# A perceiver stack on one core: the last stage's routing, gather and expert loop written anew

## What is computed

```python
logits = x_flat @ router_w
probs = jax.nn.softmax(logits, axis=-1)
expert_idx = jnp.argmax(probs, axis=-1)
gate = jnp.take_along_axis(probs, expert_idx[:, None], axis=1)[:, 0]
onehot = jax.nn.one_hot(expert_idx, E, dtype=jnp.float32)
pos_all = jnp.cumsum(onehot, axis=0) - 1.0
...
keep = (pos < C).astype(x_flat.dtype)
expert_in = expert_in.at[expert_idx, pos_c].add(x_flat * keep[:, None])
hidden = jax.nn.gelu(jnp.einsum('ecd,edf->ecf', expert_in, w1))
expert_out = jnp.einsum('ecf,efd->ecd', hidden, w2)
y = expert_out[expert_idx, pos_c] * (gate * keep)[:, None]
```

## Time and profile before

| | us |
|---|---|
| median of three runs | 3121.58 |
| the three runs | 3120.87, 3121.58, 3126.13 |
| the profiled execution's own time | 3123.37 |
| its span, first to last instruction | 3121.6 |
| PE busy | 2864.2 (92%) |
| DVE busy | 1296.2 (42%) |
| ACT busy | 973.7 (31%) |
| POOL busy | 258.0 (8%) |
| mean granted TensorE clock | 0.958 of full |

### The profile page before, as it was taken

One profiled execution on the slowest core, in us unless ns is written; L12 is line 12 of the kernel. 1 busy time (PEld: TensorE's weight loads), 2 busy tenths in 40 slices (PEclk: granted clock), 3 DMA queues, 4 the chain that ended last, 5 costly groups with the idle time before them and its releaser, 6 DMA issues.

```text
span 3121.6 us, 36422 instructions
## 1 busy us (share of the span) xinstructions
PE 2864.2 (92%) x15622; PEld 1990.0 (64%) x15622; DVE 1296.2 (42%) x1968; ACT 973.7 (31%) x1468; POOL 258.0 (8%) x267
## 2 busy tenths in 40 slices
PE   7977899898898799999999969999999999987887
PEld 3335446356583488888888847877877877844422
DVE  4355463557630633333333334254244244346211
ACT  3233223125331343343433323243233233232110
POOL 1110110221000000000000011101101101000000
PEclk9988999998899899999999979999999999988899
DMA  8872894951021122222222210100100110021197
GB/s 358 305 278 96 327 378 181 362 194 49 14 98 51 55 108 95 95 98 104 95 95 95 94 45 21 45 24 21 44 25 21 44 40 13 17 115 49 70 421 295
DMA packets 63051, 385.16 MB, mean 123 GB/s; under 512 B 6144, under 2 KB 12544, under 8 KB 33328
## 3 DMA queue, kind: packets, MB, share of 16 engines
q1 hardware_dynamic: 26640, 190.57, 16.2%
q0 software_dynamic: 29776, 188.15, 15.6%
q10 hardware_dynamic: 6480, 4.20, 0.4%
HBM read 377.63 MB, written 5.26 MB: 123 GB/s over the span
## 4 chain that ended last, share of the span: by engine, by line
PE 78%; DVE 9%; DMA 6%; ACT 5%; issue 2%; POOL 1%; SPq 0%; DVEq 0%; ACTq 0%; POOLq 0%
PE PS L420 10%; PE PS L422 10%; PE PS L421 10%; PE PS L299 4%; PE PS L607 4%; PE PS L1692 4%; PE PS L1673 3%; PE PS L580 3%; PE PS L1656 3%; PE PS L1675 3%; PE PS L1674 3%; PE PS L1658 3%; PE PS L1657 3%; DMA ring<-in_experts 2%; PE PS L1709 2%; DMA PR<-in_ctxN 2%
## 5 line engine op out<-in xcount | busy, mean ns | idle before, releaser
L420 PE MATMUL PS<-X_high,W_high 128*128 128x512 f32 x576 | 226.6, 393 | 11.0 <-DVE X_low L1151 11.0
L421 PE MATMUL PS<-X_low,W_high 128*128 128x512 f32 x576 | 225.8, 392 | 0.0
L422 PE MATMUL PS<-X_high,W_part 128*128 128x512 f32 x576 | 225.8, 392 | 0.0
L420 PE MATMUL PS<-H_high,W_high 128*128 128x512 f32 x576 | 224.2, 389 | 0.0
L422 PE MATMUL PS<-H_high,W_part 128*128 128x512 f32 x576 | 224.1, 389 | 0.0
L421 PE MATMUL PS<-H_low,W_high 128*128 128x512 f32 x576 | 224.1, 389 | 0.0
L1098 DVE TENSOR_TENSOR W_part<-ring,W_high 128x2048 fp32r<-128x2048 f32 x63 | 147.0, 2334 | 182.2 <-ACT W_high L1094 182.2
L1094 ACT ACTIVATE W_high<-ring 128x2048 fp32r<-128x2048 f32 x72 | 137.0, 1914 | 260.3 <-PE PS L422 260.3
L1856 DVE TENSOR_TENSOR RB<-PS,rows 128x512 f32<-128x512 f32 x104 | 71.9, 691 | 307.2 <-PE PS L1675 307.2
L1137 DVE TENSOR_TENSOR H_low<-T,H_high 128x512 fp32r<-128x512 f32 x144 | 99.4, 691 | 210.4 <-ACT H_high L1124 210.3
L1656 PE MATMUL PS<-C_high,W_part 128*128 128x384 f32 (+2 forms) x512 | 177.4, 347 | 4.9 <-DVE W_part L1828 4.9
(11 more groups left out here) (320 smaller groups left out, 5568.2 us busy)
## 6 DMA issues: line engine op xcount, KB each, us to landing
ring<-in_experts SPq DMA_DIRECT2D x96, 1024.0 KB, 4.8
ring<-in_tiles SPq DMA_DIRECT2D x39, 1024.0 KB, 4.8
RC<-in_ctxN POOLq DMA_DIRECT2D x24, 1536.0 KB, 11.6
RA<-in_ctxT POOLq DMA_DIRECT2D x20, 1536.0 KB, 7.0
T<-in_ctxN POOLq DMA_DIRECT2D x24, 1024.0 KB, 14.6
RA<-in_experts SPq DMA_DIRECT2D x24, 1024.0 KB, 13.0
RA<-in_ctxT POOLq DMA_DIRECT2D x12, 1666.0 KB, 13.3
RB<-in_ctxT POOLq DMA_DIRECT2D x12, 1666.0 KB, 15.7
```

The costliest lines, as they stand in the source:

```text
L420: pe.matmul(ps, a, xh, start=start, stop=False)
L421: pe.matmul(ps, a, xl, start=False, stop=False)
L422: return pe.matmul(ps, b, xh, start=False, stop=stop)
```

## The change

The router's logits are made the other way round: its weights (32 columns, padded) are stationary and 128 tokens stream, four token tiles side by side in the array; DVE copies the 128 x 128 result, PE turns it once. ACT, no longer DVE, copies the turned tokens, twice (`XTH` in fp32r and `XF` in full), and POOL, which had no work in this stage, subtracts them (`XTL`). The position sums are two matmuls of 32 columns, with `ahead6` (sums of earlier one-hots, made by DVE). The choice is made from the logits, and the gate weights come behind the selections. The gather takes two fp32r passes, 32 matmuls, token tile by token tile. The loop is gone; `hidden` reads `EIN` itself. `hidden(i + 1)` is in two halves with the transposes of step i between them, and it runs on from one pair into the next, for which the tiles are loaded in the order `ORDER6`. `SELG` is turned in the first step. Each pair is combined and added during the next one, in banks 5 to 7. The store is in four parts. In stage 3 the same helper makes the logits; they are turned behind the second hidden product of the first expert and used from there.

The core of the diff:

```diff
+        ORDER6 = []
+        for i in range(FS * E_ // 2 + 2):
+            ORDER6 += [(*divmod(i, FS), "a")] if i < FS * E_ // 2 else []
+            ORDER6 += [(*divmod(i - 1, FS), "b")] if 1 <= i <= FS * E_ // 2 else []
+        ORDER6 = [(j, f"{ab}{x}", k) for j, x, ab in ORDER6 for k in (0, 1)]
+        PLACE6 = {w: n for n, w in enumerate(ORDER6)}
...
-        def gate_pe(pe, at, tag, x, w, after, k=0):
-            for due in at.last(*after):
-                pe.wait_ge(*due)
+        def gate_pe(pe, at, tag, x, w, ready, k):
             if bank_reader.get(k):
                 pe.wait_ge(*at.done(bank_reader[k]))
-            for tt in range(T // P):
-                for c in range(KC):
-                    mm = pe.matmul(PS[:, k, tt * E_:(tt + 1) * E_], x[:, c, tt * P:(tt + 1) * P], gw[:, w, c, :],
-                                      start=(c == 0), stop=(c == KC - 1))
-            mm.then_inc(*at.step(f"{tag}.logits"))
+            for c in range(KC):
+                if c < len(ready):
+                    pe.wait_ge(*at.done(ready[c]))
+                for u in range(NTG):
+                    mm = pe.matmul(PS[u * HD:(u + 1) * HD, k, 0:P], gw[:, (w * KC + c) * E_:(w * KC + c) * E_ + HD], x[:, c, u * P:(u + 1) * P], start=(c == 0), stop=(c == KC - 1))
+            mm.then_inc(*at.step(f"{tag}.sums"))
...
+        def gate_turn_pe(pe, at, tag, k):
+            pe.wait_ge(*at.done(f"{tag}.sums.out"))
+            pe.transpose(PS[:, k, P:2 * P], MEAN, C["ident"]).then_inc(*at.step(f"{tag}.logits"))
             bank_reader[k] = f"{tag}.logits.out"
+        def gate_turn_dve(dve, at, tag, k):
+            dve.wait_ge(*at.done(f"{tag}.sums"))
+            dve.tensor_copy(MEAN, PS[:, k, 0:P]).then_inc(*at.step(f"{tag}.sums.out"))
+        def gate_logits(k):
+            return PS[:, k, P:2 * P].rearrange("p (a e) -> p a e", e=HD)[:, :, 0:E_]
...
+                          {0: lambda: gate_pe(pe, at, "s3.g", X3, 0, chunk_steps("s3.x4."), 4), 1: lambda: gate_turn_pe(pe, at, "s3.g", 4), 2: gates_turned} if i == 0 else None, {} if i else {(2, 3): "s3.gT.out"})
...
+        def s6_pool(pool, at):
+            for tt in range(4):
+                pool.wait_ge(*at.done(f"s6.xf{tt}"))
+                pool.tensor_tensor(XTL[:, tt, :], XF[:, tt, :], XTH[:, tt, :].bitcast(FP32), ALU.subtract).then_inc(*at.step(f"s6.xl{tt}"))
...
+            gate_pe(pe, at, "s6.g", N6, 1, chunk_steps("s6.ln.done."), 0)
+            tokens_turned(0)
+            gate_turn_pe(pe, at, "s6.g", 0)
+            for tt in (1, 2, 3):
+                tokens_turned(tt)
...
+            pe.matmul(POS6, C["earlier"], oh, start=True, stop=False)
+            mm = pe.matmul(POS6, C["ones"], ahead6, start=False, stop=True)
+            mm.then_inc(*at.step("s6.pos"))
...
+                pe.wait_ge(*at.done(f"s6.sel{tt}"))
+                pe.wait_ge(*at.done(f"s6.xl{tt}"))
+                for dc in range(KC):
+                    pe.matmul(bank(dc), XTH[:, tt, dc * P:(dc + 1) * P], SELR[:, tt, :], start=(tt == 0), stop=False)
+                    mm = pe.matmul(bank(dc), XTL[:, tt, dc * P:(dc + 1) * P], SELR[:, tt, :], start=False, stop=(tt == 3))
+                    if tt == 3:
+                        mm.then_inc(*at.step(f"s6.ein{dc}"))
...
+            def hidden_turned(i):
+                pe.wait_ge(*at.done(f"s6.h{i}.out"))
+                if i >= 2:
+                    pe.wait_ge(*at.done(f"s6.ht{i - 2}.out"))
+                for c in range(KC):
+                    mm = pe.transpose(PS[:, 2 + i % 2, c * P:(c + 1) * P], HS[i % 2][:, c * P:(c + 1) * P], C["ident"])
+                mm.then_inc(*at.step(f"s6.ht{i}"))
...
+            def combine(j):
+                pe.wait_ge(*at.done(f"s6.ys{j}"))
+                for dc in range(KC):
+                    k = side_bank()
+                    pe.wait_ge(*at.done(f"s6.selt{j}.out"))
+                    pe.matmul(bank(k), YS[:, j, dc * P:(dc + 1) * P], SELT[:, j, :], start=True, stop=True).then_inc(*at.step(f"s6.part{j}.{dc}"))
+                    bank_reader[k] = f"s6.part{j}.{dc}.out"
+            hidden(0, (0, 1, 2, 3))
+            for i in range(STEPS6):
+                if i + 1 < STEPS6:
+                    hidden(i + 1, (0, 1))
+                hidden_turned(i)
+                if i + 1 < STEPS6:
+                    hidden(i + 1, (2, 3))
+                if i == 0:
+                    for j in range(3):
+                        choice_turned(j)
+                if i and i % FS == 0:
+                    combine(i // FS - 1)
+                output(i)
+                if i == 0:
+                    choice_turned(3)
+            combine(E_ // 2 - 1)
...
+                act.wait_ge(*at.done(f"s6.xt{tt}"))
+                act.activation(XTH[:, tt, :], bank(4 + tt), ACT.Copy).then_inc(*at.step())
+                act.activation(XF[:, tt, :], bank(4 + tt), ACT.Copy).then_inc(*at.step(f"s6.xf{tt}"))
...
-            gate_dve(dve, at, "s6.g", False)
-            for tt in range(4):
-                dve.wait_ge(*at.done(f"s6.xt{tt}"))
-                dve.tensor_copy(XT[:, tt, :], bank(4 + tt)).then_inc(*at.step(f"s6.xt{tt}.out"))
+            gate_turn_dve(dve, at, "s6.g", 0)
...
+            dve.tensor_tensor(ahead6[:, 2:4, :], oh[:, 1:3, :], oh[:, 0:2, :], ALU.add).then_inc(*at.step())
+            dve.tensor_copy(ahead6[:, 1, :], oh[:, 0, :]).then_inc(*at.step())
+            dve.wait_ge(*at.own())
+            dve.tensor_tensor(ahead6[:, 3, :], ahead6[:, 3, :], oh[:, 0, :], ALU.add).then_inc(*at.step("s6.onehot"))
+            dve.tensor_tensor(ga, ga, bc(gst[:, 0:4]), ALU.subtract).then_inc(*at.step("s6.g.sub"))
...
+            def add_part(j):
+                for dc in range(KC):
+                    dve.wait_ge(*at.done(f"s6.part{j}.{dc}"))
+                    if j:
+                        dve.wait_ge(*at.done(f"s6.part{j - 1}.{dc}.out"))
+                    dve.tensor_tensor(X[:, dc, :], X[:, dc, :], bank(5 + (4 + 4 * j + dc) % 3), ALU.add).then_inc(*at.step(f"s6.part{j}.{dc}.out"))
+            for i in range(STEPS6):
+                j, s = divmod(i, FS)
+                dve.wait_ge(*at.done(f"s6.ht{i}"))
+                dve.tensor_copy(HT[i % 2], PS[:, 2 + i % 2, :].rearrange("p (c s) -> p c s", c=KC)).then_inc(*at.step(f"s6.ht{i}.out"))
+                if j and s == 0:
+                    add_part(j - 1)
+                if s == FS - 1:
+                    dve.wait_ge(*at.done(f"s6.y{i}"))
+                    dve.tensor_copy(YS[:, j, :], bank(4)).then_inc(*at.step(f"s6.ys{j}"))
+            add_part(E_ // 2 - 1)
+            at.same("x6")
...
+                sync.wait_ge(*at.done(f"s6.part{E_ // 2 - 1}.{c}.out"))
+                sync.dma_start(t["out"][:, c, :], X[:, c, :]).then_inc(*at.load("out_stored", "stored"))
+            sync.wait_ge(sems["out_stored"], 16 * KC)
```

More of the change, by code:

```diff
@@ L2064, in s6_pe @@
[L2064 to L2070 removed]
+                bank_reader[k] = f"s6.xf{tt}"
+            gate_pe(pe, at, "s6.g", N6, 1, chunk_steps("s6.ln.done."), 0)
@@ L2081, in s6_act @@
[L2081 to L2084 removed]
+                act.activation(SELT[:, j, :], bank(5 + j % 3), ACT.Copy).then_inc(*at.step(f"s6.selt{j}.out"))
+            for i in range(2, STEPS6):
+                gelu(i)
         def s6_dve(dve, at):
+            dve.memset(ahead6[:, 0, :], 0.0).then_inc(*at.step())
```

236 lines of the change are left out of this document (102 added, 134 removed).

## The result

The changed kernel takes 3098.84 us (median of 10 runs, 3090.82 to 3115.49). The kernel before, run beside it, takes 3125.12 (median of 10 runs; nine lie between 3120.15 and 3127.31, and one, of over 10000, was disturbed and is left out of the ratio). The ratio is 0.9913, 95% interval 0.9900 to 0.9926: 27.2 us less, with 23 to 31 as the interval. The forecast was 32.8 us less and 3088.8 us, with a range up to 3097.0, so sign and most of the size are right and the time lies 1.8 us outside the range. Part of that is the base: the forecast set out from 3121.6, and the longer series puts the kernel before at 3125.1. The part to explain is 32.8 against 27.2.

The account below looks back on a forecast made before the run. The last stage was taken as head, DMA-bound weight stream of 141 us, and tail, with only head and tail counting in full. Head 19.6, tail 13.2 and stage 3 0 made 32.8 off 3121.6, so 3088.8 us, range 3081.5 to 3097.

Parts of the forecast that it names:

- I take the same: Last stage's gather: 3.6 us at the 1.2 GHz level, as in the old gather, making 9.1 us in all.
- The lock: Last stage's head: POOL's subtractions and VectorE's small instructions hold each other up, taken as 2.5 us, bounds 0 and 4.2.
- Nothing counted: Weight stream, first pair: the turned choices (1.9) delay the second product, but no time was added for it.
- the 0.8 for the half products: Tail: transposes of product 15 inside hidden product 16, their copy behind its second half, 0.8 us less.
- the forecast of 0: Stage 3: sums 2.4 us less, PE's stop of about 2.2 takes it back; net 0, bounds -2.4 and +1.
- Head, 19.6: Last stage up to the first freed weight tiles: free at 2934.9 against 2954.54, 19.6 us earlier.
- Rival A: Cold gather: TensorE at 1.2 GHz for all 32 matmuls, 13.8 instead of 9.1; 4.8 later, 3093.6 us; chance 0.20.
- rival B: Free head: no real POOL-VectorE lock, full clock at gather's start, stage 3 gains 2; 3082.5 us; chance 0.16.
- Stream, 141 as before: Last stage's weight stream stays 141 us, bound by DMA; PE needs 35.1 a pair against 39.7 of weights.
- Rival D: Combining matmuls in the stream delay freed tiles until DMA runs dry: up to 10.5, 3099 us; chance 0.06.
- Tail, 13.2: Last weights to store: 0.8 for half products, 10.5 for combining matmuls, 1.9 for the store, together 13.2 us less.
- Rival C: Last stage without its loop: code fetches behind weight transfers stop PE or SP; at four stops 3141 us; chance 0.03.

Follow-up runs that it names:

- run 1: Changed kernel, but POOL's four subtractions wait for the last selection and the gather makes all high passes before the low ones; 3091.08 us, ratio 0.9878 to the kernel before.
- run 9: Changed kernel with the old gather: one token copy, fp32 selections, 16 fp32 matmuls, no POOL work in the stage; 3099.43 us, ratio 0.9909 to the kernel before.
- run 6: Changed kernel plus unread transposes, 36 ahead of the one-hots and 14 between position sums and first selection; 3094.76 us, ratio 0.9906 to the kernel before.
- run 7: Changed kernel with all pairs' combining matmuls and additions behind the last output product again; 3102.93 us, ratio 0.9918 to the kernel before.
- run 4: Changed kernel with late POOL, high passes first, stage 3's gates in bank 7, first step's second hidden product whole, choices turned over four steps; 3090.01 us, ratio 0.9877.
- run 8: Changed kernel with every hidden product whole ahead of the transposes; 3095.93 us, ratio 0.9892 to the kernel before.
- run 10: Changed kernel with late POOL, high passes first, stage 3's sums and turn in bank 7, every hidden product whole; 3088.75 us, ratio 0.9878 to the kernel before.
- Run 2: Changed kernel with stage 3's gate sums and turned logits in bank 7 instead of bank 4; 3098.61 us, ratio 0.9902 to the kernel before.
- run 5: Changed kernel plus 14 unread transposes while PE waits for the one-hots; 3096.04 us, ratio 0.9894 to the kernel before.

## Where the prediction was right and where it failed

Four steps failed, and a fifth was off without moving the time at N. The cold stretch of the gather was taken over from the old kernel ("I take the same": 3.6 us assumed, 5.9 measured). The lock was put too low (2.5 against 3.4). For the first pair of weights "Nothing counted" stood where the split product cost 1.3. And the 0.8 for the half products at the end did not come. In stage 3 the clock behind the stop, 1.7, was left out, and only luck in stage 4 made the forecast of 0 come true up to N. From stage 3's gate sums on the marks give 28.85 of the 32.8; the ratio's 27.2 doesn't differ from that beyond its interval.

**Head, 19.6 against 18.05.** The start of the gather was 10.6 behind the norm by the forecast and is 10.9. Two errors cancel in that: the chain without POOL was put at 8.1 and takes 7.54 (runs 1 and 9), the lock was put at 2.5 and takes 3.4. The step "two waits of 0.9 before the one-hots' sums are complete, one or two more behind them partly hidden by PE" is the mis-sized one. There were three ahead of the position sums, (1.14 - 0.19) + (1.18 - 0.17) + (1.11 - 0.17) = 2.9, and 0.5 more behind. Two things end within 0.15 us of each other there, at about 2926.9: the position sums at 1.2 GHz and the fourth wait (1.23). In run 6 the sums ran at full clock, the fourth wait took 1.24 and N to G was the same 10.97, so speeding up the sums alone would have given nothing. A small reading error changed nothing: 2.89 against 2.48 for four instructions is 0.10 each, not the 0.13 of the text, and the sum used 0.9 a wait. Each hold was nearly the whole of POOL's subtraction (1.26), not the 1.05 of its streaming. The Trainium skill (SBUF — State Buffer, "Who interferes with whom"), by whose sentence the prediction worked out about 4, was nearer than the value that was taken; the trace agrees with the full hold.

The gather was put at 9.1 and took 10.26. The failed step is "I take the same": the cold stretch of the old gather, 3.6 us, was copied over to a gather with another past. The granted clock had been full until 2924.4, and fell because the lock made PE idle; 5.9 us were cold. The price of the cold, counted with matmuls of 0.226 and 0.43, was right: 2.3 us more of it at half speed are 1.2, all that is missing. Lock and clock had been treated as two terms. They are one chain.

Rival A, cold to the last matmul, didn't come true, and that transposes can't bring the full clock is refuted: in the changed kernel the clock rose while transposes ran (2921), and in run 6 it stayed up on nothing but transposes for 4 us. The Trainium skill (TensorE: Matmul & The Clock Gate, Part 4, PE-mode transpose) has it that they don't count; these traces disagree. What A got right is that waiting ahead of the gather matters. Run 1 built rival B's free head: 5.7 us, of which B's sum had 4.3 (lock and clock).

**Stream, 141 as before.** The DMA stayed busy, combining and all: right, as run 7 shows, as far as equal streams agree (1.3 us). Rival D, combining that holds weights back, is out with that. Wrong was "nothing counted" for the first pair. The transposes between the halves of the second hidden product put off its last tiles by 0.74 us (4.17 against 3.43), and behind them the share fell to 0.64 for 2 us. At that moment nothing but the first pair is under way: all eight tiles loaded ahead have landed (share 0.00 until F), and 2 MB last 5 us at 418 GB/s. The step missed is that the second pair of requests paces the stream at its start, too, not the first alone; "six tiles queued" was no cover there, since the six were tiles in place, not requests.

**Tail, 13.2 against 10.8.** The matmuls (14.02 to 3.71) and the store came as forecast, 12.0 against 12.4. The 0.8 for the half products did not come, and 1.2 were lost instead, 2.0 in all. Runs 4, 8 and 10 lay 1.3 of them to the split in the first step (0.5 to 2.0): with that step whole, the last output product begins 143.1 to 143.3 behind F, where the two traces of the old code have 143.45 and 143.09. The forecast took the old chain and shortened one link; but the product ahead of the last now waits for weights (3082.25), so what the halves save ahead of it is only a longer wait.

**Stage 3, 0 against +1.6, and 0 up to N.** The sums (2.55 less), the turn (0.27) and the stop (2.12) are all within 0.2 of the forecast. The term left out is what the stop does to the clock: 1.7 us of work lost in the 3.4 us at 1.2 GHz behind it. Run 2 removes both. That the changed kernel is level again at N (1807.2 us from the gate sums in both) is luck: the clock came back sooner in stage 4, and nothing in the forecast's working stood for that.

**Code fetch.** Rival C is out: in the last stage, with no loop, five packets of code were fetched from 2940 us on, no wait of PE by issue stands out, and the slower side never came near. The Trainium skill (Runtime: NRT & Kernel Launch, Instruction fetch mechanics) says that straight code is fetched ahead; nothing here contradicts it.

**The base.** The three runs shown lay 3.5 us below the median of the longer series. The range was laid around a time, while the forecast was about a difference: 3125.1 - 32.8 is 3092.3, and 3121.6 - 27.2 = 3094.4 would have been inside. The difference of 32.8 itself is above the measured interval (23 to 31), so the base is not the whole of the miss.

## What to carry to other kernels

A wait that a change puts ahead of TensorE has two prices: the wait itself, and the clock behind it (stops of 2.1 and 3.4 us brought it down here); count both, or fill the whole wait with transposes. Work on an engine that was idle in a stage isn't free if it holds up the engine on the critical path: start it behind the last link of that chain, even where that looks late. When stretches between marks are added up, take all of them: a sum that leaves one out can agree with the total by chance. Where transfers bound a stretch, the order of work inside it counts at its start, when few requests are out: look at when the first two or three go out.

## What the hardware showed that was not expected

- VectorE instructions of 4 to 32 columns, 0.16 to 0.19 us alone, took 1.11 to 1.23 beside POOL's 512-column subtractions of 1.26. A copy of 8 columns that began where one subtraction ended and the next began took 0.16 in the changed kernel and 1.29 in run 5, so a small shift in time can add a whole wait.
- A stop of PE of 2.1 us, behind 21 us at full clock, was followed by 3.4 us at 1.2 GHz.
- The granted clock stayed at 1.00 through 4 us of nothing but transposes (run 6). With an idle piece of 1.8 us ahead of the gather (run 1) it did not fall, with one of 3.4 us (the changed kernel) it did.
- With four stores of 256 KB the span ended 2.8 us behind the last addition, against 4.3 behind the issue of one store of 1 MB: 1.5 less, where the bandwidth alone had promised 1.9.
